# Attention inputs split on GpSimd and turned by DMA transposes, with three maximum banks and two score banks

## The reference

```python
# x: [16,512,256], context: [16,1601,256], of which the causal mask leaves the first 512 tokens
q = layernorm(x) @ Wq.T;  k = context @ Wk.T;  v = context @ Wv.T        # 16 heads of 16
scores = where(causal, q @ k.T / 4, -inf);  y = softmax(scores) @ v
x = x + tanh(g_xattn) * (y @ Wo.T + bo)
n = layernorm(x)
affinity = softmax(n @ gate_w.T)            # 8 experts, each takes its top 128 tokens a batch
x = x + tanh(g_ffn) * scatter_add(gating * expert(n[idx]))
```

## Time and profile before

| | |
|---|---|
| time, 3 runs | 2071.72 us median (2069.85 to 2073.26) |
| profiled execution | 2071.41 us, its span 2069.4 us |
| TensorE's granted clock, mean | 0.974 |
| busy share of the span | PE 91%, DVE 57%, ACT 45%, POOL 28% |
| DMA | 221.51 MB, mean 107 GB/s |

### The profile page before, as it was taken

The page is one execution under the profiler, slowest core; times in us unless marked ns, Lnnn a source line. Parts: engine busy times, 40 slices in busy tenths (PEclk is TensorE's granted clock), DMA queues, the critical chain, the costliest instruction groups (busy, mean ns, idle before and its releaser), DMA issues.

```text
span 2069.4 us, 42083 instructions
## 1 busy us (share of the span) xinstructions
PE 1888.7 (91%) x14056; PEld 1121.2 (54%) x14056; DVE 1178.8 (57%) x2825; ACT 931.6 (45%) x1780; POOL 582.8 (28%) x492
## 2 busy tenths in 40 slices
PE   3899999999999999998189999999999999999997
PEld 1455555555555555554036656556555565565665
DVE  4777788787788887875743343443434434334332
ACT  2355555555555555555143343343433434434332
POOL 2122222222222222221323233233232332423322
PEclk9799999999999999999589999999999999999999
DMA  3534444444444443342755466454663546534412
GB/s 112 114 114 115 118 116 124 138 141 129 138 119 132 130 133 111 118 127 72 200 110 100 82 113 120 82 95 87 125 109 77 94 88 125 107 62 81 73 26 26
DMA packets 311030, 221.51 MB, mean 107 GB/s; under 512 B 193016, under 2 KB 292480, under 8 KB 310912
## 3 DMA queue, kind: packets, MB, share of 16 engines
q1 hardware_dynamic: 286336, 186.35, 36.1%
q0 software_dynamic: 24576, 33.57, 10.2%
HBM read 118.63 MB, written 58.72 MB: 86 GB/s over the span
## 4 chain that ended last, share of the span: by engine, by line
PE 46%; DVE 2%; DMA 2%; issue 1%; POOL 0%; ACT 0%; DVEq 0%; POOLq 0%
PE bank L1001 10%; PE bank L1002 10%; PE bank L1003 10%; PE bank L1019 5%; PE bank L1017 5%; PE bank L1018 5%; DMA out<-y,row_now 1%; DVE top_at L1070 1%; DVE work L1073 1%; DVE top L1068 1%; POOL out L961 0%; DVE h L1108 0%; ACT y L1055 0%; DMA rows<-tokens,row_now 0%; POOL rows L953 0%
## 5 line engine op out<-in xcount | busy, mean ns | idle before, releaser
L534 ACT ACTIVATE prob<-bank 128x512 f32<-128x512 f32 x640 | 372.1, 596 | 237.4 <-PE bank L423 229.8
L961 POOL DMA_INDIRECT out<-y,row_now x128 | 201.6, 1575 | 658.1 <-ACT y L1055 633.7
L1108 DVE TENSOR_TENSOR h<-bank,silu 128x512 f32<-128x512 f32 x256 | 176.2, 688 | 339.9 <-PE bank L1003 317.5
L403 PE MATMUL bank<-ks,qs 96*128 96x128 bf16 (+3 forms) x1024 | 282.1, 308 | 65.7 <-DVE mx L622 40.4
L622 DVE CUSTOM_DVE_ANT_0 masked<-bank,causal 128x384 f32<-128x384 f32 (+1 forms) x512 | 304.1, 616 | 45.4 <-PE bank L403 43.9
L1047 ACT ACTIVATE h<-h 128x512 bf16<-128x512 f32 x256 | 161.2, 630 | 347.6 <-DVE h L1108 327.3
L1111 DVE TENSOR_TENSOR h<-h 128x512 bf16<-128x512 f32 x256 | 177.2, 692 | 179.4 <-ACT h L1047 175.7
L1019 PE MATMUL bank<-downT,h 128*128 128x256 bf16 x1024 | 279.1, 273 | 0.0
L1018 PE MATMUL bank<-downT,h 128*128 128x256 bf16 x1024 | 279.1, 273 | 0.0
L1017 PE MATMUL bank<-downT,h 128*128 128x256 bf16 x1024 | 279.1, 273 | 0.0
L421 PE MATMUL bank<-qs,ks 98*128 98x512 bf16 (+3 forms) x1024 | 268.8, 302 | 0.1
(11 more groups left out here) (146 smaller groups left out, 2821.6 us busy)
## 6 DMA issues: line engine op xcount, KB each, us to landing
qs<-q_parts SPq DMA_DIRECT2D x384, 64.0 KB, 2.6
ks<-k_parts SPq DMA_DIRECT2D x384, 64.0 KB, 2.8
q_parts<-q_sb SPq DMA_DIRECT2D x32, 384.0 KB, 3.1
k_parts<-k_sb SPq DMA_DIRECT2D x32, 384.0 KB, 3.2
x_t<-in_x SPq DMA_DIRECT2D x16, 512.0 KB, 4.1
ctx_t<-in_ctx SPq DMA_DIRECT2D x16, 512.0 KB, 4.9
res_t<-in_x SPq DMA_DIRECT2D x16, 512.0 KB, 5.6
out<-x SPq DMA_DIRECT2D x16, 512.0 KB, 3.2
```

The costliest lines, as they stand in the source:

```text
L403: last = nc.tensor.matmul(dst[:, h * w:(h + 1) * w], qs[0:STACK, gr, h0 + h, i * P:(i + 1) * P], ks[0:STACK, gr, h0 + h, 0:w], start=True, ...
L534: nc.scalar.activation(prob[:, gr % 2, h0:h0 + nh, POFF[tiles[0]]:POFF[tiles[0]] + w], sc_bank[SC_BANK[k]][:, 0:nh * w].rearrange("p (h w) ...
L961: nc.gpsimd.indirect_dma_start(out_rows, bass.IndirectOffsetOnAxis(ap=row_now[:, par, CHUNK * c + s:CHUNK * c + s + 1], axis=0), y[:, c % ...
```

## The change

- `xn` and `ctx_t` are no longer turned by TensorE. GpSimd splits them where they lie, tokens on the partitions, into hi and lo bf16 parts `x_nat` and `c_nat`, each in two halves of the tokens (a copy that rounds, then a subtraction; "xsplit" at (0, 1) and (0, 2), "csplit" at (0, 6)). SyncE then issues four DMA transposes a batch, two at (0, 5) into `xT` ("xturn") and two at (0, 10) into `cT` ("cturn"), behind the loads of group 2; each turns 128 x 1024 bf16. `xT` and `cT` are laid out by token tile first; q's and k's matmuls read them in four pieces of 128 columns.
- "tx", "tx+", "tc" and "tc+" go from TensorE, ScalarE and VectorE. The second half of "ln1+" moves from (0, 5) to (0, 1).
- The copy to `v_aug` moves from VectorE to GpSimd, at the same place of the order.
- Three banks hold maxima and two hold scores. A maximum unit waits for the unit three before it (in the first two positions of a batch two before it), each score unit for the exponential two before it.

```diff
-SC_BANK = [0, 1, 2, 0, 1, 2, 0, 1, 2, 1]
-SC_BEFORE = [6 - NSC, 9 - NSC, 8 - NSC, 0, 1, 2, 3, 4, 5, 7]
+SC_BANK = [k % 2 for k in range(NSC)]
+SC_BEFORE = [k - 2 for k in range(NSC)]
+def max_at(gr, k):
+    return (gr * NMAX + k) % 3
+def max_ahead(gr, k):
+    return 1 if gr == 0 and k < 2 else 2
...
-        0: {0: [("pv", b - 1, 1, 0), ("ln1+", b + 1, 0)], 1: [("yt", b - 1, 0), ("pv", b - 1, 1, 1)],
-            2: [("yt+", b - 1, 0), ("yb", b - 2, 1)],
+        0: {0: [("pv", b - 1, 1, 0), ("ln1+", b + 1, 0)],
+            1: [("yt", b - 1, 0), ("pv", b - 1, 1, 1), ("xsplit", b + 1, 0), ("ln1+", b + 1, 1)],
+            2: [("yt+", b - 1, 0), ("yb", b - 2, 1), ("xsplit", b + 1, 1)],
...
-            5: [("pv", b - 1, 1, 3), ("o+", b - 2, 0), ("o", b - 2, 0, 0), ("o", b - 2, 0, 1), ("ln1+", b + 1, 1)],
-            6: [("pv+", b - 1, 1)],
-            7: [("o", b - 2, 1, 0), ("o", b - 2, 1, 1), ("o+", b - 2, 1), ("tx", b + 1, 0), ("tx+", b + 1, 0)],
-            9: [("tx", b + 1, 1), ("tx+", b + 1, 1)], 10: [("yt", b - 1, 1), ("stack", b, 2)]},
+            5: [("pv", b - 1, 1, 3), ("o+", b - 2, 0), ("o", b - 2, 0, 0), ("o", b - 2, 0, 1), ("xturn", b + 1)],
+            6: [("pv+", b - 1, 1), ("csplit", b + 1, 0), ("csplit", b + 1, 1)],
+            7: [("o", b - 2, 1, 0), ("o", b - 2, 1, 1), ("o+", b - 2, 1)],
+            10: [("yt", b - 1, 1), ("stack", b, 2), ("cturn", b + 1)]},
...
-            7: [("pv", b - 1, 2, 2), ("tc", b + 1, 0), ("tc+", b + 1, 0)], 8: [("mrow", b, 0), ("tc", b + 1, 1)],
+            7: [("pv", b - 1, 2, 2)], 8: [("mrow", b, 0)],
...
-        max_bank, sc_bank, pv_bank, job_bank = bank[0:2], bank[2:5], bank[5], bank[6:8]
+        max_bank, sc_bank, pv_bank, job_bank = bank[0:3], bank[3:5], bank[5], bank[6:8]
...
+                elif kind in ("xturn", "cturn"):
+                    n = kind[0]
+                    hold(split_lo[n], count(b, 2, 2))
+                    hold(filled["q" if n == "x" else "v"], count(b, 2, 0))
+                    src, dst = (x_nat, xT) if n == "x" else (c_nat, cT)
+                    for r in range(2):
+                        sp.dma_start_transpose(dst[:, r, :, :, :].rearrange("p i d c -> p (i d) c"),
+                                               src[:, r, :, :].rearrange("p i d -> p (i d)")).then_inc(flipped[n], 16)
...
-                    wait(pe, max_read, n - 1)
+                    wait(pe, max_read, n - max_ahead(gr, k))
...
+                elif kind in ("xsplit", "csplit"):
+                    n, half = kind[0], p[2]
+                    if n == "x":
+                        wait(pool, ln_done["ln1"], count(b, NT, 2 * half + 2))
+                    else:
+                        wait(pool, ctx_loaded, count(b, 16, 16))
+                    wait_apart(pool, flipped[n], count(b, 32, 0), passed["pool"])
+                    src, dst = (xn, x_nat) if n == "x" else (ctx_t, c_nat)
+                    src, at = src[:, 2 * half:2 * half + 2, :], slice(2 * half, 2 * half + 2)
+                    nc.gpsimd.tensor_copy(dst[:, 0, at, :], src).then_inc(split_hi[n], 1)
+                    wait(pool, split_hi[n], count(b, 2, half + 1))
+                    nc.gpsimd.tensor_tensor(out=dst[:, 1, at, :], in0=src, in1=dst[:, 0, at, :], op=ALU.subtract)\
+                        .then_inc(split_lo[n], 1)
...
+                elif kind == "vaug":
+                    wait(pool, pv_filled, count(b, GROUPS, 0))
+                    wait_apart(pool, read["v"], count(b, 2, 2), passed["pool"])
+                    nc.gpsimd.tensor_copy(v_aug[:, :, :, 0:HD],
+                                          v_new[:, :, :].rearrange("p i (h d) -> p i h d", h=HEADS))\
+                        .then_inc(vaug_done, 1)
```

More of the change, by code:

```diff
@@ L186, in attention @@
     xn = sb(ctx, "xn", [P, NT, D], F32)
[L187 to L188 removed]
+    x_nat = sb(ctx, "x_nat", [P, 2, NT, D], BF16)
+    c_nat = sb(ctx, "c_nat", [P, 2, NT, D], BF16)
+    xT = sb(ctx, "xT", [P, 2, NT, NH2, P], BF16)
+    cT = sb(ctx, "cT", [P, 2, NT, NH2, P], BF16)
     parts = {"q": sb(ctx, "q_sb", [P, 3, NH2, T], BF16), "k": sb(ctx, "k_sb", [P, 3, NH2, T], BF16)}
@@ L450, in piece @@
                     last.then_inc(filled[kind], 1)
-                elif kind in ("yb", "tx", "tc", "xt"):
+                elif kind in ("yb", "xt"):
                     half = p[2]
-                    src = {"yb": yq, "tx": xn, "tc": ctx_t, "xt": xn2}[kind]
+                    src = {"yb": yq, "xt": xn2}[kind]
                     if kind == "yb":
                         wait(pe, read["yt"], count(b, GROUPS, 2 * half + 2))
[L456 to L459, removed]
                     else:
@@ L467, in piece @@
                     t = p[2]
-                    src, made = (xT, "tx") if kind == "q" else (cT, "tc")
+                    src, made = (xT, "x") if kind == "q" else (cT, "c")
                     if p[3] == 0:
-                        wait(pe, read[made], count(b, 2, 2))
+                        wait(pe, flipped[made], count(b, 32, 32))
                     for n in range(3 * p[3], 3 * p[3] + 3):
                         c, rw, rs = PRODUCTS[n]
-                        last = nc.tensor.matmul(to[:, :], wT["w" + kind][:, rw, c, t * P:(t + 1) * P],
-                                                src[:, rs, c, :], start=(n == 0), stop=(n == len(PRODUCTS) - 1))
+                        last = nc.tensor.matmul(to[:, :].rearrange("p (i t) -> p i t", i=NT), wT["w" + kind][:, rw, c, t * P:(t + 1) * P],
+                                                src[:, rs, :, c, :], start=(n == 0), stop=(n == len(PRODUCTS) - 1))
                     if p[3] == 1:
@@ L477, in piece @@
                 elif kind in ("v", "o"):
-                    src, made = (cT, "tc") if kind == "v" else (ynT, "yb")
                     if p[3] == 0:
-                        wait(pe, read[made], count(b, 2, 2))
+                        if kind == "v":
+                            wait(pe, flipped["c"], count(b, 32, 32))
+                        else:
+                            wait(pe, read["yb"], count(b, 2, 2))
                     i2, i = p[3], 2 * p[2] + p[3]
                     for n, (c, rw, rs) in enumerate(PRODUCTS):
-                        last = nc.tensor.matmul(to[:, i2 * D:(i2 + 1) * D], src[:, rs, c, i * P:(i + 1) * P],
+                        src = cT[:, rs, i, c, :] if kind == "v" else ynT[:, rs, c, i * P:(i + 1) * P]
+                        last = nc.tensor.matmul(to[:, i2 * D:(i2 + 1) * D], src,
                                                 wT["w" + kind][:, rw, c, :], start=(n == 0),
@@ L677, in piece @@
                 elif kind == "ln1+":
-                    wait(dve, filled["tx"], count(b, 2, 0))
+                    wait(dve, split_lo["x"], count(b, 2, 0))
                     norm_apply("ln1", xn, x_t, b, p[2])
@@ L687, in piece @@
                     norm_apply("ln2", xn2, x1, b, p[2])
[L688 to L693, removed]
-                        .then_inc(vaug_done, 1)
                 elif kind == "lt+":
```

28 lines of the change are left out of this document (15 added, 13 removed).

## The result

| | before | after |
|---|---|---|
| time | 2071.3 us median of 4 (2069.85 to 2073.26) | 2012.2 us median of 4 (2008.71 to 2017.19) |
| profiled execution, span | 2069.4 us | 2006.9 us |

The ratio is 0.971, 95% interval 0.9696 to 0.9725: 59 us, 2.9% faster. 2011 us was forecast.

The account below looks back on a forecast made before the run. TensorE was taken to bound the kernel. Per batch 1.76 (transposes) + 2.9 (maximum waits) - 0.4 (score banks) = 4.3 us; 15 batches give 64, less 4 at the start: 2071.4 - 60 = 2011 us, range 1993 to 2052.

Parts of the forecast that it names:

- TensorE sets the pace: In the loop TensorE is busy 562.96 of 600 us; work taken from it comes back unless something else becomes late.
- all on the engine that sets the pace: Four sets of transposes a batch on TensorE, 0.44 us each: removing them gains 1.76 us a batch.
- Third maximum bank: TensorE's waits for VectorE to empty maximum banks nearly all go: 2.9 of 3.2 us a batch, bounds 0 and 3.2.
- The first rival: VectorE, still 80% busy, or the score banks give the gain back: only 20 us gained, 2051 us; chance 0.17.
- Two score banks: Score units on TensorE wait a little for exponentials: costs 0.4 us a batch, bounds 0 and 2.4.
- The tightest case before: In the old trace a score unit starts at 406.59; the exponential two before it ends at 406.49.
- GpSimd: Splits and copy (1.6 us taken, 1.04 to 2.4) raise it from 14.2 to about 23 us a batch, all hidden.
- SyncE's queue: Transposes take 3.0 us a pair, slack 1.8 at group 0's scores; rival: 7.8 a pair, 2120 us, chance 0.06.
- The rival's limit: On SyncE, loss exceeds gain from rows 4.3 us late: a pair of 6.4 us, 3.2 us an instruction.
- Transfer by blocks: Rival: a pair's 16 blocks move serially, 1.3 us each, 21 us; q comes late, about 2210 us; chance 0.04.
- The start: At program start q begins at 27 to 30, first stacked loads come some 4 us later, bounds 1 and 8.
- a sign that the prediction named: If right, TensorE never waits for xT or the rows from m_sb; q's matmuls waiting for xT would show it wrong.

Follow-up runs that it names:

- extra_two: Changed kernel with two more DMA transposes of 128x1024 behind each pair, into a spare tile nobody reads: 2094.2 us, ratio 1.0098.
- early_y: Changed kernel with half of yq split on GpSimd at (1, 7) and turned by two DMA transposes at (1, 8): 2110.6 us.
- half_y: Changed kernel, group 3's maxima turned at (0, 5), half of yq split on GpSimd at (2, 3) and DMA-turned at (2, 5): 2022.8 us.

## Why the prediction was right

**TensorE sets the pace: right, but not alone.** The terms of the sum were 1.76 for transposes, 2.9 for waits, less 0.4. The measured 4.4 us a batch is their 4.3, and no wait for a maximum is left in the loop. What the sum hid is that its terms are not separate. Alone, the parts give 25, 12 and 14 us, 51 together; as a whole 59. Left out last, they are worth 34 (banks), 17 (copy) and 17 us (transposes). The periods say it more sharply: 1.3, 0.7 and 0.9 us a batch alone, 2.9 together, and 4.4 as a whole. The transposes were costed as "all on the engine that sets the pace", because at 401.00 TensorE ran on without a wait. With two banks that was no proof: a few units further on TensorE meets a bank that VectorE has to empty. Half of the 1.76 us was lost until the third bank was there, and with it 1.6 came through.

**Third maximum bank: right, some 3.2 rather than 2.9.** All the waits for maxima went. The added 0.16 us for each wait, from the spacing of two matmuls, was needed: the view's own 2.4, less the new wait of 0.4, would have left the sum 0.6 short. That part of the sum is an account, not an experiment. The first rival (VectorE at 80% gives it back) did not come, though VectorE is at 80% still: its idle time was bridged.

**Two score banks: over-costed.** 0.4 us was taken; the trace shows 0.13, at one unit a batch, and none beside two maximum banks. The tightest case before (0.10 us to spare) was near the truth.

**GpSimd: right on its own time, not on VectorE's.** The copy took 1.04 us, the lower bound, not 1.6. Neither q nor pv waited for GpSimd in the loop; 126.7 us more in all where 140 was forecast. VectorE is 56.4 us less busy where 68 was forecast, because the first layer norm became 13.8 us longer beside the split. The prediction had read from the copy to `v_aug` that VectorE is held while GpSimd works, and still said that no other term changes: but half of "ln1+" now stands right next to the new split. The new wait of 0.4 us a batch at (0, 4), which was not forecast, follows it in the trace. That the sum gave 4.3 for 4.4 is in part luck: this 0.4 was missing, while the score banks were costed 0.3 too high and the third maximum bank 0.3 too low.

**SyncE's queue: right in mechanism, price too low.** A pair took 2.64 us (3.0 taken) and landed 4.5 us after its start by the medians (7 taken). That left 2.6 us at the scores of group 0 where 1.8 was forecast. The rival's limit was put at a pair of 6.4 us, from where on the loss would exceed the gain; a pair made 5.3 us long already ran slower than before. The prediction had no term for the clock: a wait of 2.9 us brought another 2.4 us a batch at a granted clock of 0.50, and 5.3 is more than the 4.4 gained.

**Transfer by blocks: as the trace said.** The 16 blocks of a pair landed 4.5 us after the first issue, against at most 7.2 by the rows before. The Trainium skill, "VectorE: DVE Perf Modes", section "The three transpose paths", gives 1309 ns for one block by DMA. One after another 16 would be 21 us, an estimate from that page's figure; here, with eight blocks in an instruction, they landed in 4.5, so the figure doesn't add up block by block, and the measurement decides.

**The start: 4 us forecast, none at the scores, and that by chance.** q began 4.3 us later (28.19 for 23.88), but k only 1.8 (34.15 for 32.31): the prediction had k's matmuls at q's slow pace too, and the twelve took 2.75 us before and 2.76 after where q's took 4.86 and 4.54. The profile grants 1.00 in both stretches, so what makes q's slow stays open. The first maximum unit starts 1.3 us later (53.94 for 52.60). The first score matmul starts at 75.4 us in both traces, yet for different reasons: before, TensorE came to it through waits for VectorE's maxima, and after it stood 2.20 us for the row pieces, whose "mrow" is issued at 72.92 behind a pair of transposes and not at 67.00. TensorE waiting for `xT` or for the rows from `m_sb`, a sign that the prediction named, came up at the start only (9.48 and 2.20 us). From there to the last score matmul is 824.7 us in place of 889.4, 64.7 less (forecast: 64); what comes after it is 2.2 longer, and the span 62.5 shorter.

## What to carry to other kernels

An engine that is 94% busy does not make every microsecond taken from it count: look at what the next wait on its path hangs on, and give it room (here one PSUM bank) before or together with taking its work away. Measure each part with and without the others: alone, the transposes seemed worth half of what they were. Price an extra buffer by its tightest use in the trace, not by the count of its users. Before work goes to an engine that slows another, look at what the other does at that moment. In a queue that issues for everyone, a transfer's cost is its issue time plus what slides behind it; and a wait of TensorE can cost more than its length: one of 2.9 us cost 5.3 here, with the lower clock behind it.

## What the runs showed of the hardware that was not expected

- A DMA transpose of 128x1024 bf16 held SyncE for 1.3 us, hardly longer than one of 128x512 (1.26 us), and landed 3.2 us after its issue.
- TensorE waits of 2.84 us (extra_two) and 4.93 us (early_y) were followed by 4 and 3 us at a granted clock of 0.50 (in extra_two with two more at 0.70), one of 2.03 us (half_y) by a stretch of 2 us at 0.51.
- With three loads of 512 KB issued just ahead of it, a store of 384 KB landed in 6.8 us (early_y); with 4 us between them it landed in 3.2.
- GpSimd's copy of 128x1024 fp32 to scattered places took 1.04 us, the same as its dense rounding copy; VectorE's took 0.69 alone and 1.56 beside GpSimd's subtraction.
- Two scaling instructions of VectorE (128x256 fp32, the layer norm) took 0.73 us alone and 1.73 beside GpSimd's copy and subtraction.
